# Softmax attention over 16 heads: two alternating pairs of PSUM banks for the scores, probabilities transposed in two halves through one bank

## What is computed

```python
# block 1: block-sparse cross attention of LN(x) on ctx: 16 heads of 8
h = (x @ W.T).reshape(B, S, 16, 8)            # q from LN(x), k and v from ctx
scores = einsum('qd,kd->qk', q, k) * 8**-0.5  # with 64 rows to a sequence: one block
out = softmax(scores) @ v ... @ Wo.T
# block 2, twice (L = 2): causal self attention, then a mixture of 8 experts, top 2
x = x + _attn(_ln(x, ...), wq, wk, wv, wo, bq, bk, bv, bo)   # 16 heads of 8, causal
x = x + moe(_ln(x, ...), ...)
```

## Time and profile before

| | |
|---|---|
| median of 3 runs | 1461.72 us (1461.04 to 1464.89) |
| the profiled execution | 1459.84 us, its span 1458.2 us |
| cross attention | about 47 to 209 us |
| self attention 0 | about 231 to 400 us |
| self attention 1 | about 721 to 888 us |
| TensorE busy over the whole span | 1045.8 us (72%) |
| VectorE, ScalarE, GpSimd | 888.6, 682.3, 671.7 us (61%, 47%, 46%) |

### The profile page before, as it was taken

One profiled execution on the slowest core, in us unless ns is written; L12 is line 12 of the kernel. 1 busy time (PEld: TensorE's weight loads), 2 busy tenths in 40 slices (PEclk: granted clock), 3 DMA queues, 4 the chain that ended last, 5 costly groups with the idle time before them and its releaser, 6 DMA issues.

```text
span 1458.2 us, 33401 instructions
## 1 busy us (share of the span) xinstructions
PE 1045.8 (72%) x9572; PEld 822.7 (56%) x9572; DVE 888.6 (61%) x2034; ACT 682.3 (47%) x1690; POOL 671.7 (46%) x1091
## 2 busy tenths in 40 slices
PE   1699965999758999900199995289995887899003
PEld 1477743777558999900167772167774665688001
DVE  0699976999757666612389993622225111776895
ACT  0477744777520777700177773255552112577103
POOL 6355523666301444367366661133331454898213
PEclk9999986999955999955599995589998555999555
DMA  3000030000020222211310000000000000011001
GB/s 100 12 15 14 19 112 1 2 0 0 1 58 8 60 64 64 58 50 52 110 28 0 0 1 0 0 1 0 0 0 2 20 22 18 26 40 43 0 0 58
DMA packets 49178, 38.67 MB, mean 27 GB/s; under 512 B 6408, under 2 KB 41716, under 8 KB 49124
## 3 DMA queue, kind: packets, MB, share of 16 engines
q1 hardware_dynamic: 42372, 27.75, 6.4%
q0 software_dynamic: 4320, 8.86, 2.3%
q10 hardware_dynamic: 2432, 1.40, 0.4%
HBM read 29.13 MB, written 8.85 MB: 26 GB/s over the span
## 4 chain that ended last, share of the span: by engine, by line
PE 60%; DVE 12%; issue 7%; POOL 7%; POOLq 6%; ACT 4%; DMA 1%; DVEq 1%; another core or an unknown queue 1%; ACTq 0%; SPq 0%
PE ps_s L921 12%; PE ps_o L921 11%; PE ps_a L921 10%; PE ps_v L921 7%; PE ps_t L1005 6%; PE ps_t L921 5%; POOLq L604 4%; PE ps_x L957 3%; PE ps_v L1028 2%; POOL work L605 2%; POOL h_all L574 2%; POOL w L574 1%; PE ps_x L949 1%; DVE stats L1275 1%; POOLq L594 1%
## 5 line engine op out<-in xcount | busy, mean ns | idle before, releaser
L545 POOL TENSOR_TENSOR kbd<-kts,kmask 128x512 f32<-128x512 f32 x192 | 240.9, 1277 | 257.1 <-ACT qts L729 171.4
L957 PE MATMUL ps_x<-ident,xn 128*128 128x128 f32 x160 | 59.8, 374 | 163.9 <-DVE xn L1307 153.8
L567 POOL DMA_INDIRECT xg<-x_rows,row_from x71 | 69.0, 972 | 156.3 <-DVE slot_of L1480 83.2
L1316 DVE TENSOR_REDUCE rowmax<-ps_s 128x16 f32<-128x1024 f32 x96 | 116.5, 1213 | 24.2 <-PE ps_s L921 24.2
L957 PEld LDWEIGHTS ps_x<-ident,xn 128*128 128x128 f32 x160 | 26.8, 168 | 178.6 <-DVE xn L1307 148.1
L754 ACT COPY probs_t<-ps_t 128x1024 f32<-128x1024 f32 x96 | 97.2, 1012 | 62.2 <-PE ps_t L1005 62.2
L1320 DVE TENSOR_TENSOR work<-ps_s,rowmax 128x1024 f32<-128x1024 f32 x96 | 117.6, 1225 | 3.3
L921 PE MATMUL ps_o<-vst,probs_t 128*64 128x18 f32 x3072 | 107.7, 213 | 7.7 <-ACT probs_t L754 7.7
L921 PEld LDWEIGHTS ps_o<-vst,probs_t 128*64 128x64 f32 x3072 | 98.1, 138 | 20.2 <-ACT probs_t L754 10.1
L921 PE MATMUL ps_s<-kbd,qts 64*64 64x512 f32 x768 | 105.1, 618 | 1.8 <-DVE work L1320 1.4
L1005 PE MATMUL ps_t<-ident,work 128*128 128x128 f32 x768 | 101.9, 277 | 1.7 <-ACT work L745 1.7
(11 more groups left out here) (349 smaller groups left out, 2636.9 us busy)
## 6 DMA issues: line engine op xcount, KB each, us to landing
y_rows<-work SPq DMA_DIRECT2D x71, 64.0 KB
ctx_in<-in_ctx_dram SPq DMA_DIRECT2D x64, 64.0 KB, 1.8
w<-in_L_ffn_e_w_dram SPq DMA_DIRECT2D x2, 2048.0 KB, 9.4
ctx_dup<-in_ctx_dram SPq DMA_DIRECT2D x64, 64.0 KB, 2.2
x_rows<-h_all SPq DMA_DIRECT2D x1, 2048.0 KB, 8.7
out_dram<-work SPq DMA_DIRECT2D x16, 128.0 KB, 1.8
xg<-x_rows,row_from POOLq DMA_INDIRECT x71
b2b<-in_L_ffn_e_b_dram ACTq DMA_DIRECT2D x1, 512.0 KB
```

The costliest lines, as they stand in the source:

```text
L545: i = pool.tensor_tensor(km[:, par, g, :, :], kts[:, par, g:g + 1, :].to_broadcast([P, 8, SEQ]), kmask[:, :, :], ALU.mult)
L567: pool.indirect_dma_start(xg[:, t % XBUFS, :], None, x_d, bass.IndirectOffsetOnAxis(row_from[:, t:t + 1], 0)).then_inc(xg_loaded[t % XBUFS ...
L957: nc.tensor.transpose(ps_x[:, 0:P], xn[:, par, :], ident[:, :]).then_inc(S["xt_ready"], 1)
L1316: V.tensor_reduce(rowmax[:, par, :], s3, AXX, ALU.max).then_inc(S["max_ready"], 1)
```

## The change

- `ps_s` and `ps_t` become one tensor of four banks, `ps_st`. In the softmax attentions the scores of even and odd tiles go to its first and second pair; the scores wait for the subtraction two tiles back.
- The probabilities are transposed in two halves of four transposes, both through bank `ps_x`. ScalarE copies each half out. Half 1 waits for the copy of half 0. The weighing is split into two halves too, and on TensorE the output projection stands between them.
- The transposes of xn and ctx go to `ps_v`, columns 256 to 511, beside y's transpose and the output; they wait until the output of an earlier tile has been read, and y's transpose waits for an earlier copy of xn.
- The lists that set the order on TensorE and ScalarE are rewritten. The mLSTM attention and the expert stages keep their work; only semaphore counts are renamed.

```diff
-        ps_s = psum("ps_s", 1024)
-        ps_t = psum("ps_t", 1024)
+        ps_st = psum("ps_st", 2048)
+        ps_s, ps_t = ps_st[:, 0:1024], ps_st[:, 1024:2048]
+        ps_sc = [ps_st[:, b * 1024:(b + 1) * 1024].rearrange("p (r n) -> p r n", r=GROUPS) for b in range(2)]
+        def HALF(base, t, k=0):
+            return 2 * (ATT[base] + t) + k
+        def xcol(base):
+            return (ps_x, 0) if base in ("p1", "m") else (ps_v, 2 * P)
...
             def evac_pt(base, k):
-                    nc.scalar.copy(probs_t[:, par, :], ps_t[:, :]).then_inc(S["pts_ready"], 1)
+                    nc.scalar.copy(probs_t[:, par, k * 512:(k + 1) * 512], ps_x[:, :]).then_inc(S["pts_ready"], 1)
...
             def attention(base, l):
-                pipeline(act, [(L_OUT, evac_yt(base)), (L_WEIGH, evac_pt(base)), (2, evac_qkv(base, l), VBUFS),
-                               (1, evac_t(base, l, None if l is None else 0, l is None)),
-                               (L_SCORES, exp_step(base))])
+                pipeline(act, [(L_WEIGH, evac_pt(base, 0)),
+                               (1, evac_t(base, l, None if l is None else 0, l is None)), (L_OUT, evac_yt(base)),
+                               (L_WEIGH, evac_pt(base, 1)), (L_SCORES, exp_step(base)),
+                               (2, evac_qkv(base, l), VBUFS)])
...
             def transposes(base, nbase):
+                    if base not in ("p1", "m"):
+                        seen(pe, S["x_updated"], UPD[base] + t - 5)
+                    bank, at = xcol(base)
...
             def scores(base, masked):
-                    seen(pe, S["shifted_ready"], ATT[base] + t)
+                    seen(pe, S["shifted_ready"], ATT[base] + t - 1)
...
-            def transpose_probs(base):
+            def transpose_probs(base, k):
-                    seen(pe, S["pts_ready"], ATT[base] + t)
-                    for j in range(HEADS // 2):
-                        i = nc.tensor.transpose(ps_t[:, j * P:(j + 1) * P], probs[:, par, j * P:(j + 1) * P], ident[:, :])
+                    seen(pe, S["pts_ready"], HALF(base, t, k))
+                    for j in range(HEADS // 4):
+                        at = k * 512 + j * P
+                        i = nc.tensor.transpose(ps_x[:, j * P:(j + 1) * P], probs[:, par, at:at + P], ident[:, :])
...
-                    pe.wait_ge(S["pts_ready"], ATT[base] + t + 1)
+                    pe.wait_ge(S["pts_ready"], HALF(base, t, k + 1))
-                    for j in range(HEADS // 2):
+                    for j in range(4 * k, 4 * k + 4):
...
             def transpose_y(base):
+                    pe.wait_ge(S["xts_ready"], TB[base] + capped(t + L_OUT - 1, NT))
...
-                pipeline(pe, [(L_SCORES, scores(base, l is not None)),
-                              (L_OUT, transpose_y(base)), (L_WEIGH, transpose_probs(base)),
-                              (2, project(base, l))]
-                             + early + [(1, transposes(base, nbase)), (L_OUT, out_project(base, l)),
-                                        (L_WEIGH, weigh(base), VBUFS)])
+                pipeline(pe, [(L_SCORES, scores(base, l is not None)), (L_WEIGH, transpose_probs(base, 0)),
+                              (L_OUT, transpose_y(base))]
+                             + early + [(1, transposes(base, nbase)), (2, project(base, l)),
+                                        (L_WEIGH, transpose_probs(base, 1)), (L_WEIGH, weigh(base, 0), VBUFS),
+                                        (L_OUT, out_project(base, l)), (L_WEIGH, weigh(base, 1), VBUFS)])
```

More of the change, by code:

```diff
@@ L26 @@
 L_SCORES, L_WEIGH, L_OUT = 4, 5, 6
+GROUPS = 2
+HPG = HEADS // GROUPS
 VBUFS = 4
@@ L148, in build @@
         ones_b = sb("ones_b", [P, P], BF16)
-        kmask = sb("kmask", [P, 8, SEQ])
+        kmask = sb("kmask", [P, HPG, SEQ])
         kmask4 = sb("kmask4", [P, 4, SEQ])
@@ L466, in _ @@
             fresh(pool.memset(ones_b[:, :], 1.0))
-            for buf, hh, hd, width in ((kmask, 8, HD, SEQ), (kmask4, 4, MHD, SEQ)):
-                for half in range(2):
-                    part = buf[half * 64:(half + 1) * 64, :, :]
+            for buf, hh, hd, width, rows_ in ((kmask, HPG, HD, SEQ, 64), (kmask4, 4, MHD, SEQ, 64)):
+                for half in range(P // rows_):
+                    part = buf[half * rows_:(half + 1) * rows_, :, :]
                     fresh(pool.memset(part, 1.0))
@@ L704, in fn @@
                         seen(act, S["ht_stored"], t - 1)
+                    bank, at = xcol(base)
                     if vk is None:
-                        i = nc.scalar.copy(xcts[:, par, :, :].rearrange("p a k -> p (a k)"), ps_x[:, 0:2 * P])
+                        i = nc.scalar.copy(xcts[:, par, :, :].rearrange("p a k -> p (a k)"), bank[:, at:at + 2 * P])
                     else:
-                        i = nc.scalar.activation(xts[:, par, :], ps_x[:, 0:P], ACT.Identity,
+                        i = nc.scalar.activation(xts[:, par, :], bank[:, at:at + P], ACT.Identity,
                                                  bias=vec(vk + 1, l), scale=vec(vk, l))
@@ L743, in fn @@
                     act.wait_ge(S["shifted_ready"], ATT[base] + t + 1)
-                    seen(act, S["pt_ready"], ATT[base] + t - 1)
+                    seen(act, S["pt_ready"], HALF(base, t - 1))
                     nc.scalar.activation(probs[:, par, :], shifted[:, par, :], ACT.Exp, scale=HD ** -0.5
@@ L867, in evac_ctil @@
             def evac_ctil(t, par):
[L869 removed]
+                act.wait_ge(S["pt_ready"], PT_M + t + 1)
                 seen(act, S["o_ready"], ATT["m"] + t - 1)
@@ L948, in fn @@
                     pe.wait_ge(ctx_loaded[par], (8 * NT if base == "m" else 0) + arrived(t, par, 16))
-                    nc.tensor.transpose(ps_x[:, P:2 * P], ctx_in[:, par, :], ident[:, :]).then_inc(S["ctx_used"], 1)
+                    if base == "x":
+                        seen(pe, S["x_updated"], UPD[base] + t - 5)
+                    bank, at = xcol(base)
+                    nc.tensor.transpose(bank[:, at + P:at + 2 * P], ctx_in[:, par, :], ident[:, :]).then_inc(S["ctx_used"], 1)
                 return fn
@@ L956, in fn @@
                     seen(pe, S["xts_ready"], TB[base] + t)
-                    nc.tensor.transpose(ps_x[:, 0:P], xn[:, par, :], ident[:, :]).then_inc(S["xt_ready"], 1)
+                    if base not in ("p1", "m"):
+                        seen(pe, S["x_updated"], UPD[base] + t - 5)
+                    bank, at = xcol(base)
+                    nc.tensor.transpose(bank[:, at:at + P], xn[:, par, :], ident[:, :]).then_inc(S["xt_ready"], 1)
                 return fn
@@ L1019, in fn @@
                                    vst[:, slot, s, j, :, :].rearrange("p g d -> p (g d)"))
-                    i.then_inc(S["o_ready"], 1)
+                    if k == 1:
+                        i.then_inc(S["o_ready"], 1)
                 return fn
@@ L1204, in transpose_ctil @@
                 pe.wait_ge(S["ctil_ready"], t + 1)
-                seen(pe, S["pts_ready"], ATT["m"] + t - 1)
+                seen(pe, S["pts_ready"], PT_M + t - 1)
                 for j in range(MH // 2):
@@ L1211, in weigh16 @@
             def weigh16(t, par):
-                pe.wait_ge(S["pts_ready"], ATT["m"] + t + 1)
+                pe.wait_ge(S["pts_ready"], PT_M + t + 1)
                 pe.wait_ge(S["vb16_ready"], t + 1)
@@ L1661, in ctil_step @@
                 dve.wait_ge(S["scores_ready"], ATT["m"] + t + 1)
-                seen(dve, S["pt_ready"], ATT["m"] + t - 1)
+                seen(dve, S["pt_ready"], PT_M + t - 1)
                 V.tensor_tensor(ctil[:, par, :].rearrange("p (r n) -> p r n", r=2), ps_s3[:, :, 0:4 * SEQ],
```

36 lines of the change are left out of this document (19 added, 17 removed).

## The result

| | before | changed |
|---|---|---|
| median | 1461.38 us (4 runs) | 1503.51 us (1502.31 to 1504.64, 4 runs) |
| ratio | | 1.028 (95% interval 1.0267 to 1.0293) |
| span of the profiled execution | 1458.2 us | 1503.0 us |
| TensorE busy over the span | 1045.8 us | 1085.4 us |

The kernel is slower by 42 us, where 19.6 were forecast (1481). The side was right and the range (1464 to 1518) holds the time, but the loss is twice the size.

A forecast was written before the change was run, and what follows sets the result against it. The prediction took TensorE to be the bound, nearly full. Banks -3, split +22, loop's end +4, fill and drain -4, the rest 0, gave +19 us, 1481 us as a median, with a range of 1464 to 1518.

The forecast's parts named there:

- What bounds it: Steady turns of the three 16-head attentions: TensorE is the bound, with 0.3 to 0.4% of its time free.
- The banks, -3 us: Two pairs of score banks remove a TensorE wait of 0.09 in some 32 self-attention turns: -3 us.
- The split, +22 us: Weighing split around the output projection adds one wide and one narrow run on TensorE: 0.26 a turn, 84 turns, +22 us.
- A: Rival, faster: gaps at changes of form are waiting, not cost, so the split is free: 1452 us, chance 0.10.
- The halves, 0: Probabilities transposed in halves through one bank: ScalarE's half copies end in time for TensorE, 0, at most 0.1 a turn.
- xn into y's and the output's bank, 0: xn on VectorE starts at 0.68, before GpSimd's mask multiply at 0.95 of the turn, and takes 0.35: 0.
- B: Rival, slower: xn caught behind the mask multiply, TensorE waits 0.5 or more; 1523 us, in every second turn 1502; chance 0.12.
- It corrects itself: Argument against B: a later exp pushes GpSimd's mask multiply later too.
- The loop's end, +4 us: TensorE's branch is hidden behind only the last 8 weighings instead of 16: 18 turns, 0.2 more each, +4 us.
- Fill and drain, -4 us: Last turns of each attention: halves overlap copy and transposes, gaining about 1.2 in two turns, some lost before: -4 us.
- D: Rival: the terms cancel, the extra narrow run is free and only the wide one's 0.15 is paid: 1465 us, chance 0.05.
- C: Rival, slower: serial handshakes, TensorE's register loads and the halves' copies cost 0.3 a turn together: 1506 us, chance 0.13.

The follow-up runs named there:

- run 6: Changed kernel with xn before y on VectorE and the output projection before an unbroken weighing: 1460.06 us, ratio 0.9982; the same with one pair of score banks: 1461.85 us, 1.0.
- run 1: Changed kernel with VectorE normalising xn before it divides y: 1477.89 us against 1455.96, ratio 1.0141.
- run 4: Kernel before, with only the weighing cut into two runs of eight pairs and the output projection put between them: 1502.26 us, ratio 1.031.
- run 5: Changed kernel with the output projection put in front of the weighing, which stays in one run of 16 pairs: 1464.32 us, ratio 1.0055.
- run 3: Changed kernel with GpSimd's mask multiply for tile t held until xn of tile t+2 is done: 1480.48 us against 1462.11, ratio 1.0127.
- run 7: Kernel before, with xn in front of y on VectorE and nothing else: 1469.17 us, ratio 1.0049.
- run 2: Changed kernel with GpSimd's mask multiply for tile t held until xn of tile t+1 is done (the wrong tile): 1495.58 us, ratio 1.0266.

## Why the prediction was right or wrong

**What bounds it: right.** TensorE was full, and run 6 without the second pair of banks has the same steady turns. **The banks, -3 us: too much.** The wait of 0.09 was put on every second self turn; in the trace of before it is on every fourth (4.69, 4.77, 4.69, and 4.81 with the branch), 12 turns or so, 1 us.

**The split, +22 us: right, a little small.** 0.30 a turn where 0.26 was taken (0.19 to 0.31 given). The out projection on its own takes 0.42 (332.03 to 332.45), not 0.37: the term of the sum that was low is the head of the wide run, 0.10 instead of 0.06. Weighing 0, out and weighing 1 together take 1.57 (331.46 to 333.03), over the 1.4 that was to be the sign of A. One reading beside it was wrong: between y's transpose and the first of the probabilities' there is a gap in the earlier trace rows, 0.17 where two wide starts are else 0.109 apart; it is the head that the sum itself had priced. By totals, run 1 less run 6 is 1.59%, 23 us.

**The halves, 0: right.** A copy of 512 columns takes 0.58 to 0.59, as the line between the two rows said. Run 1's steady turns are 0.30 over those of before in both kinds of attention, which is the split alone (run 4), so the halves add nothing there. Only where the output projection goes first (run 5) does half 1 come 0.05 late.

**xn into y's and the output's bank, 0: wrong, and the whole miss.** This is the step that failed: "xn goes first and takes 0.35". It was put at 0 and measured 20 to 22 us (22 in the steady turns). Three things in it were off. The two events were placed 0.27 apart (xn at 0.68, the multiply at 0.95 of the turn); in the trace of after xn starts at 0.74 to 0.77 in most self turns, and the multiply at 0.84 or 0.85 in two turns of four, at 0.67 and 0.54 in the others. The multiply was placed 0.1 to 0.4 too late: a margin of 0.27 at the end of so long a chain of rows is no margin. It was worked out for self attention alone; in cross attention k and q are copied faster (0.27 against 0.37) and the multiply starts at 0.57 to 0.65 in three turns of four (at 0.3 in the fourth), on top of xn or ahead of it:

```profile
105.34 1.35 DVE L1329 TENSOR_SCALAR xn<-x_res,mean,rstd 128x128 f32 x1
```

```profile
105.33 2.50 POOL L556 TENSOR_TENSOR kbd<-kts,kmask 128x512 f32<-128x512 f32 x2 [2.81 <-ACT qts L739]
```

And being first by a little does not help, see below. The step did see that xn's transpose had moved from 3.16 to 1.80 of the turn, which takes the slack away that had made a blocked xn free. That should have been priced from the rows as they stood: xn was caught in most turns before. Instead B got a chance of 0.12. Its price per caught turn was too high: xn's transpose comes at up to 2.25 instead of 1.80, 0.45, but 0.28 in the mean of the 66, where 0.5 was written. That the variant "in every second one" gave 1502, 1.5 from the measured time, is luck: more turns are caught, each for less.

**It corrects itself: half right.** The multiply's place against xn changes from turn to turn, and the turns settle in a repeating pattern (4.99, 5.56, 5.21, 5.50) rather than at 4.99. The pattern is four turns long, as is a pass of the loop; run 1, without collisions, shows a multiply moved from 0.67 or 0.75 to 0.43 to 0.45 in the turn behind the branch. So the branch has a part in it; how much, no run separates.

**The loop's end, +4 us: smaller.** Branch turns are about 0.23 longer than their neighbours in run 1, against 0.14 before, and there are 15 and not 18: 0.09 x 15, 1.4 us. **Fill and drain, -4 us** was not measured by itself: the rest of the span in the table of run 6 is 1.2 us shorter in the changed kernel and 4.8 in run 1, and a difference of 5 us also stands between the two kernels of run 6, whose steady turns are the same. Without the collision the sum of the prediction comes out, 19 forecast, 18.6 (run 3) to 20.6 us (run 1) by the ratios, but with some luck: the split (25, not 22) and the banks (-1, not -3) make it 5 us too low, the loop's end 3 too high.

**The rivals.** A and D fell in run 4's cross turns, C in runs 1 and 3. The changed kernel is the forecast plus B.

## What to carry to other kernels

When a step is moved earlier on one engine, take the durations of what it waits for as the trace shows them, blocked time included, unless the margin to the blocker is larger than the error of the whole chain behind it; a collision that costs nothing is one whose result nobody wants yet. Before giving a waiting engine more buffers, check that it waits at all, and count how often a busy TensorE changes between whole and partial arrays: putting one wide matmul pair between two narrow runs cost 0.30 us a turn, some 25 us here, without adding any work. A cheap reorder (xn first, the weighing whole) took the changed kernel from 2.8% slower to 0.2% faster. The same reorder of VectorE alone made the kernel before slower (run 7), so an order has to be checked in the kernel in which it is to stand.

## What the runs showed of the hardware that was not expected

xn (a tensor_scalar from SBUF to SBUF) is blocked by a GpSimd multiply not only when it starts later, but also when it starts up to 0.10 us earlier. In the changed kernel, with the multiply starting 0.10 or less behind xn it is caught (26 of 26, up to 0.100); from 0.104 on it escapes with 0.35. The other traces agree, with an edge that lies a little differently in each: caught up to 0.099 and free from 0.109 in run 5, caught up to 0.092 in run 2, where one at 0.096 is free, as two are in run 7. When xn escapes by so little, the multiply's first instruction is the longer one, 1.37 instead of 1.27 (328.89: the two take 2.60, and 2.50 at 323.38). The Trainium skill (SBUF — State Buffer, SBUF: two separate sides) gives the lock to whichever starts first; by the recorded starts the trace differs by this tenth of a microsecond, and the measurement decides. Whether the lock is taken later than xn's start or the start is recorded early, no row tells. The blocked xn ends 0.08 to 0.09 after the multiply's first instruction, also where the second is recorded to start 0.04 before that one's end. So xn waits for one instruction and not for both; that the lock changes hands between them is argued from this.
